# A two-layer graph network: the experts' remainder tile packed, more expert blocks kept on the chip, the second layer's gate and norms by row tile

## The reference, cut to what matters

```
x = x + gatv2(xn) + mix(xn);  x = x + experts0(layernorm(x))   # 16 experts, hidden 512, top 2
xn = layernorm(x)
# second layer: attention over the edges, then gate, norm and slope
skip = xn @ Wskip.T + bskip
g = sigmoid(concat[skip, rst, skip - rst] @ Wgate.T + bgate)    # rst: the attention's result
rst = g * skip + (1 - g) * rst
rst = layernorm(rst) * ln_w + ln_b;  rst = where(rst >= 0, rst, a * rst)
x = x + rst + (mix_out + xn)                                    # mix_out = q @ kv, 8 heads of 32
# causal attention block on layernorm(x)
x1 = layernorm(x);  h = rmsnorm(x1) * ln1_w;  q, k, v from h, with rotary positions
x2 = x1 + attention(q, k, v) @ wo.T;  flat = rmsnorm(x2) * ln2_w
out = sum over the top 2 of 8 experts of w * (silu(flat @ w1.T) * (flat @ w3.T)) @ w2.T   # hidden 682
x = x + x2 + out
```

## Time and profile before

| | us |
|---|---|
| median of 3 runs | 1204.14 |
| lowest and highest | 1200.51, 1206.46 |
| the profiled execution | 1199.38 |
| its span, first to last instruction | 1197.6 |
| PE, PEld, DVE busy | 958.0, 829.1, 857.0 |
| ACT, POOL busy | 465.5, 466.9 |

### The profile page before, as it was taken

The page is one execution under the profiler, slowest core; times in us unless marked ns, Lnnn a source line. Parts: engine busy times, 40 slices in busy tenths (PEclk is TensorE's granted clock), DMA queues, the critical chain, the costliest instruction groups (busy, mean ns, idle before and its releaser), DMA issues. The chain is left out here.

```text
span 1197.6 us, 19285 instructions
## 1 busy us (share of the span) xinstructions
PE 958.0 (80%) x6570; PEld 829.1 (69%) x6570; DVE 857.0 (72%) x1934; ACT 465.5 (39%) x791; POOL 466.9 (39%) x374
## 2 busy tenths in 40 slices
PE   4277999679989889974736999976891894999995
PEld 2256798568878778854735999864691683788884
DVE  5457459869887779887987888584879547655514
ACT  1154565557859577527511111101460260111110
POOL 2437878887787778850002222150000000211104
PEclk9688999889999999997866999997996896899998
DMA  8942232322322222129505999870000002777763
GB/s 284 292 145 69 52 73 55 83 47 60 74 62 58 61 61 69 34 44 245 142 22 192 335 322 323 319 246 22 1 2 0 1 2 71 260 268 264 268 240 93
DMA packets 58236, 157.47 MB, mean 131 GB/s; under 512 B 23830, under 2 KB 33227, under 8 KB 49907
## 3 DMA queue, kind: packets, MB, share of 16 engines
q1 hardware_dynamic: 25500, 116.04, 29.8%
q0 software_dynamic: 25056, 24.10, 9.0%
q10 hardware_dynamic: 7610, 16.46, 4.1%
HBM read 136.12 MB, written 20.12 MB: 130 GB/s over the span
## 5 line engine op out<-in xcount | busy, mean ns | idle before, releaser
L2075 POOL DMA_INDIRECT arena<-row_tab,ids x42 | 57.8, 1376 | 503.2 <-DVE ids L1528 500.6
L2030 POOL DMA_INDIRECT pair_scores<-sc_ring,idx_ring x160 | 213.6, 1335 | 61.9 <-issue 48.0
L750 PE MATMUL bank<-arena 128*128 128x128 f32 (+1 forms) x1616 | 200.6, 282 | 3.2 <-DMA arena<-in_exp 3.2
L750 PEld LDWEIGHTS bank<-arena 128*128 128x128 f32 (+1 forms) x1616 | 188.0, 190 | 12.2 <-DMA arena<-in_exp 4.4
L2020 POOL DMA_INDIRECT arena<-xl_tab,idx_ring x120 | 157.9, 1316 | 91.8 <-issue 37.5
L1763 ACT ACTIVATE arena<-fmaps,node_neg 125x875 f32<-125x875 int32 x100 | 100.2, 1023 | 33.8 <-PE bank L524 14.5
L761 PE MATMUL bank<-arena 128*128 128x256 f32 (+1 forms) x404 | 99.2, 388 | 0.5 <-DMA arena<-in_exp0o 0.5
L1767 ACT ACTIVATE late_ohT<-arena 125x875 fp32r<-125x875 f32 x100 | 90.7, 927 | 0.0
L1899 ACT ACTIVATE arena<-bank 128x512 f32<-128x512 f32 (+2 forms) x76 | 32.4, 450 | 140.9 <-PE bank L750 140.9
L524 PE MATMUL bank<-late_hi,late_ohT 125*125 125x256 f32 x500 | 84.3, 298 | 1.4 <-DVE arena L1000 0.8
L761 PEld LDWEIGHTS bank<-arena 128*128 128x128 f32 (+1 forms) x404 | 72.0, 190 | 17.3 <-issue 9.0
(11 more groups left out here) (330 smaller groups left out, 1977.0 us busy)
## 6 DMA issues: line engine op xcount, KB each, us to landing
arena<-in_exp SPq DMA_DIRECT2D x25, 1024.0 KB
arena<-in_exp SPq DMA_DIRECT2D x17, 1364.0 KB
arena<-in_exp0o SPq DMA_DIRECT2D x25, 512.0 KB
arena<-in_exp1o SPq DMA_DIRECT2D x17, 640.0 KB
fmaps<-in_rows SPq DMA_DIRECT2D x20, 437.5 KB
arena<-pair_scores SPq DMA_DIRECT2D x7, 1093.8 KB
pair_scores<-cnt SPq DMA_DIRECT2D x5, 1093.8 KB
pair_scores<-cnt ACTq DMA_DIRECT2D x5, 1093.8 KB
```

The source lines that it names most:

```text
L750: mm = pe.matmul(banks[1 + 2 * q + buf][0:rows, i * SLOTS:(i + 1) * SLOTS], w_in(s, q, k, m, rows), xsT[:, s, k, :], start=(k == 0), stop= ...
L2030: p.indirect_dma_start(out=pair_scores[which], in_=sc_ring[:, b % 2, j, :], in_offset=None, out_offset=bass.IndirectOffsetOnAxis(ap=idx_ri ...
L2075: p.indirect_dma_start(out=xs[:, q, :], out_offset=None, in_=tab, in_offset=bass.IndirectOffsetOnAxis(ap=ids[:, q, :], axis=0))\
```

## The change

1. **Packed remainder (e1).** The 42 remaining columns of w3 and of w1 stand in one weight tile of 106 columns (w3 in columns 0 to 41, zeros to 63, w1 in 64 to 105). One product of 106 columns takes the place of two of 42. ACT reads w1's part from partitions 64 up, DVE w3's from partition 0 up, in the same bank. The block's weight load grows from 2728 to 2772 columns.
2. **KEPT** is 5 in e0 and 3 in e1. The fifth matrix and result use `mask_words`, so the making of `nmask` and `cnt` moves from e0's end to behind `from_fm("xnT2")`.
3. **Gate.** The third weighted sum is folded into two (weights wg_skip + wg_diff and wg_rst - wg_diff). The skip sums move ahead in `beside_l1`; tiles 0 to 3 are gated at i = 21, with exp, add and reciprocal in place of sigmoid; only tile 4 is left for after the attention.
4. **Norms.** The affine's weight and bias are folded into the passes, x + xn is brought into `cout`'s bank by PE as an identity product, both inverse roots of the double norm are made in one pass (`norm_twice`), and tiles 0 to 2 go ahead of 3 and 4. PE turns and projects chunk 0 when tiles 0 to 2 are there, then chunk 1.
5. **Router.** The rows are multiplied with ln2_w and turned before the inverse root is known; the root is multiplied into the 8 logits on DVE and into the rows on ACT (into `te`, stored from there). x + x2 moves behind `select(3, 1)` of e1.

```diff
-KEPT = {"e0": 4, "e1": 2}
+KEPT = {"e0": 5, "e1": 3}
...
+PACKED = REST_AT + REST1
...
+                                if rows < 128:
+                                    for k in range(K2 if q == 0 else 0):
+                                        pe.matmul(banks[1 + buf][0:PACKED, i * SLOTS:(i + 1) * SLOTS],
+                                                  w_rest(s, k), xsT[:, s, k, :], start=(k == 0), stop=(k == 1))
+                                    continue
...
-            pe.wait_ge(sem("ah"), 1)
-            to_fm("ahT", ta)
-            read_out(pe, "ahT")
-            for name, tiles in (("aq", K2), ("aqr", K2), ("ak", 1), ("akr", 1)):
-                linear_fm(name, fa, name, tiles)
+            for c, (off, w, tiles) in enumerate(CHUNKS):
+                pe.wait_ge(sem("ah"), tiles[-1] + 1)
+                turned(("ahT", c), ta, c)
+                for k in range(K2):
+                    read_out(pe, "ahT", c, k)
...
-                if name == "e0":
-                    for m in range(T):
-                        own.note(v.tensor_scalar(nmask[:, m, :], cnt[:, m, :], -1.0, -BIG, ALU.is_lt, ALU.mult))
...
+                elif i == 21:
+                    gated(1, 0, 1, 2, 3)
...
+            add_prelu(0, 1, 2)
+            norm_twice(0, 1, 2)
+            add_prelu(3, 4)
+            chunk_from_fm("ahT", fa, 0)
+            norm_twice(3, 4)
+            dve.wait_ge(sem("rope_in"), 16)
+            chunk_from_fm("ahT", fa, 1)
+            roped(0)
+            roped(1)
...
+                v.tensor_tensor(ta[:, t, :], tb[:, t, :], Vt(1, "rms2"), ALU.mult).then_inc(sem("weighed"), 1)
```

More of the change, by code:

```diff
@@ L891, in _ @@
             linear_tm("ao", fa, lambda k: W("ao", k), D)
-            pe.wait_ge(sem("flat"), 1)
-            to_fm("flatT", ta)
+            for c, (off, w, tiles) in enumerate(CHUNKS):
+                pe.wait_ge(sem("weighed"), tiles[-1] + 1)
+                turned(("flatT", c), ta, c)
             read_out(pe, "flatT")
@@ L1582, in experts @@
                 select(3, 1)
+                if beside is not None:
+                    beside()
                 block_steps(dve, nblk, step)
[L1584 to L1590 removed]
                 copy_y(nblk - 1, (nblk - 1) % 2)
@@ L1610, in _ @@
             from_fm("xnT2", fa)
+            for m in range(T):
+                own.note(v.tensor_scalar(nmask[:, m, :], cnt[:, m, :], -1.0, -BIG, ALU.is_lt, ALU.mult))
+            own.fence()
+            for m in range(T):
+                own.note(v.scalar_tensor_tensor(cnt[:, m, :], cnt[:, m, :], HD ** 0.5, nmask[:, m, :], ALU.mult,
+                                                ALU.add))
             for c, (off, w, _) in enumerate(CHUNKS):
@@ new lines, in gate_logits, with gated @@
+            def gate_logits(a, b):
+                own.link(v.tensor_tensor(gate[:, a:b], gpart[:, 0, a:b], gpart[:, 1, a:b], ALU.add))
+                v.tensor_scalar(gate[:, a:b], gate[:, a:b], vec[0:P, V_BGATE:V_BGATE + 1], -80.0, ALU.add, ALU.max)\
+                    .then_inc(sem("glogit"), 1)
+            def gated(n, *tiles):
+                a, b = tiles[0], tiles[-1] + 1
+                dve.wait_ge(sem("gated"), n)
+                own.link(v.tensor_scalar(gate[:, a:b], gate[:, a:b], 1.0, None, ALU.add))
+                own.link(v.reciprocal(gate[:, a:b], gate[:, a:b]))
+                for t in tiles:
+                    own.note(v.scalar_tensor_tensor(te[:, t, :], ta[:, t, :], gate[:, t:t + 1], te[:, t, :], ALU.mult,
+                                                    ALU.add))
+                own.fence()
+                for t in tiles:
+                    own.note(v.bn_stats(stats[:, t, :], te[:, t, :]))
@@ L1637, in beside_l1, with centred @@
+            def centred(*tiles):
+                own.fence()
+                for t in tiles:
+                    own.note(v.bn_aggr(mv[:, t, :], stats[:, t, :]))
+                own.fence()
+                for t in tiles:
+                    own.note(v.scalar_tensor_tensor(ta[:, t, :], te[:, t, :], mv[:, t, 0:1], Vt(1, "ln_w"),
+                                                    ALU.subtract, ALU.mult))
             def beside_l1(i):
@@ L1673, in _ @@
                    all_tiles, lambda o, a: v.tensor_scalar(o, a, 1e-30, None, ALU.max), te, beside_l1)
[L1674 to L1677 removed]
+            gate_rest(T - 1)
+            gate_logits(T - 1, T)
             for k in range(K2):
@@ L1681, in _ @@
                     .then_inc(freed, 1)
-            dve.wait_ge(sem("gated"), 1)
-            for t in range(T):
-                own.note(v.scalar_tensor_tensor(te[:, t, :], ta[:, t, :], gate[:, t:t + 1], te[:, t, :], ALU.mult,
-                                                ALU.add))
+            centred(0, 1, 2, 3)
+            gated(2, T - 1)
+            centred(T - 1)
             own.fence()
-            layernorm(te, ta, 1e-5, (sem("ln"), 3 * T))
-            affine(ta, 1, "ln_w", "ln_b", sem("g1"))
@@ L1860, in attend, with gate_exponentials @@
                         turned_out(i - 2)
+                    if name == "l1" and i == len(steps):
+                        gate_exponentials(0, T - 1, 1)
+            def gate_exponentials(first, end, n):
+                act.wait_ge(sem("glogit"), n)
+                a.activation(gate[:, first:end], gate[:, first:end], ACT.Exp, scale=-1.0).then_inc(sem("gated"), 1)
             def elu_exponentials(m):
@@ L1955, in _ @@
             attend("l1", all_tiles)
-            act.wait_ge(sem("glogit"), 1)
-            a.activation(gate[:, :], gate[:, :], ACT.Sigmoid, bias=vec[0:P, V_BGATE:V_BGATE + 1])\
-                .then_inc(sem("gated"), 1)
-            from_fm("ahT", fa)
+            gate_exponentials(T - 1, T, 2)
+            chunks_from_fm("ahT", fa)
             attend("l2", causal_tiles)
             from_fm("yT", fa)
-            from_fm("flatT", fa)
+            chunks_from_fm("flatT", fa)
+            act.wait_ge(sem("flat_root"), 1)
+            for t in range(T):
+                a.activation(te[:, t, :], ta[:, t, :], ACT.Copy, scale=rstd[:, t:t + 1]).then_inc(sem("flat"), 1)
             shares("gate1", NE1)
```

219 lines of the change are left out of this document (147 added, 72 removed).

## The result

The changed kernel takes 1173.33 us (median of 4 runs, 1164.56 to 1175.26), the kernel before beside it 1203.12 us (1200.51 to 1206.46). The ratio is 0.9752, 95% interval 0.9718 to 0.9785: 25.9 to 33.9 us gained, 29.8 by the ratio. Predicted were 27.4 us and 1177, range 1168 to 1189. The profiled execution takes 1172.37 us, its span is 1170.5 (before 1197.6).

What follows compares the result with a forecast made beforehand. PE was taken to bound both expert stretches, DVE the stretch between the attentions. Terms -18.2 - 5.1 + 2.0 - 2.2 - 3.9 = -27.4 us on 1204.14 gave 1176.7, predicted as 1177, range 1168 to 1189.

Steps and rivals of the forecast that it cites:

- e1's end: After e1's blocks: last adds 7.8 us behind PE's outputs instead of 12.9, gathers ending last by 0.9; 5.1 us gained.
- E1's blocks: PE in e1: four fewer instructions and fewer width-change pauses gain 1.07 us a block, 18.2 us over 17 blocks.
- The bet: In e1's products, a 106-column tile counts as full, so pauses beside it vanish; 18.2 us taken.
- the pauses stay: Rival in e1's blocks: pauses remain with 106 columns, gain only 7.6 to 12.9 us, time 1182 to 1188; chance 0.20.
- Transfers: Rival in e1: blocks become bound by transfers, nothing of the 18.2 us seen, time 1195; chance 0.04.
- E0: First expert stretch: fifth kept block brings a new wait, +2.0 us, bounds -1 to +9.
- The chain: In e0, DVE waits some 10 us for fetched rows, delaying block 24's gather; PE's turning comes 3.4 us late.
- Gate, norms, projections: Between the attentions: chunk 0 turned ten us earlier, attention starts at 950.1 instead of 952.73; -2.2 us, from -5 to +1.
- The last rival of the list: Norms: tiles 0 to 2 first gain nothing for projections, chunk 0's copy waiting; costs 2 us at most, 1179.
- Router: Second attention to top 2: top 2 done at 1003.9, -3.9 us, from -4.5 to -3.

Runs made afterwards that it cites:

- experiment 11: The changed kernel with KEPT 4 instead of 5 in e0; 1169.69 us, ratio 0.9751 to the kernel before.
- experiment 1: The changed kernel with e1's remainder unpacked again into two products of 42 columns; 1182.94 us, ratio 0.9854 to the kernel before.
- experiment 5: The changed kernel with e0's two rows stored a step earlier and fetched at the end of step 3 instead of step 20's start; 1167.78 us, ratio 0.9726.
- experiment 7: The changed kernel with slope, add and double norm for all five row tiles at once, not tiles 0 to 2 first; 1170.86 us, ratio 0.9774.
- experiment 8: The changed kernel with chunk 0's rotary passes on DVE ahead of chunk 1's copy; 1168.25 us, ratio 0.9741.
- experiment 6: The changed kernel with KEPT 4 instead of 3 in e1, block 13's share left out of row tiles 0 and 2; 1168.3 us, ratio 0.9721.
- experiment 12: The changed kernel with the gate of all five row tiles behind the attention; 1173.92 us, ratio 0.9787.
- experiment 4: The kernel before with unit 1's order changed, both full products first, then both of 42 columns; 1195.4 us, ratio 0.995.
- experiment 2: The kernel before with the packed remainder alone; 1179.05 us, ratio 0.9796.

## Why the prediction was right

The forecast held, in sum and in its mechanisms; its terms were off by up to 3 us, in both directions. That e1's end gave 1.0 us less and the norms 3.2 more, so that the sum came within 2.4 us of the measured 29.8, is partly luck. By stretches, each profile cut at the same instructions (means; in brackets the profiles and their extremes):

| stretch | before | changed | difference | predicted |
|---|---|---|---|---|
| e0, first hidden product to last adds | 162.1 (5: 159.6 to 163.7) | 163.3 (7: 161.0 to 166.6) | +1.2 | +2.0 |
| to the causal attention | 147.0 (4: 145.4 to 148.0) | 141.6 (6: 140.8 to 142.2) | -5.4 | -2.2 |
| to the top 2 | 55.0 (5) | 50.4 or 52.1 | -4.6 or -2.9 | -3.9 |
| e1, first hidden product to first combining | 156.7 (2: 156.2, 157.1) | 138.9 (10: 138.1 to 139.6) | -17.8 | -18.2 |
| to the last adds | 13.2 (4: 12.9 to 13.5) | 9.1 (7: 7.7 to 11.0) | -4.1 | -5.1 |
| sum | | | -30.7 or -29.0 | -27.4 |

An experiment counts in the column of the part that it has (KEPT 4 of experiment 11 as "before" in e0, experiment 1's blocks as "before" in e1). The ratio says -29.8.

- **E1's blocks: right in mechanism and size.** The bet was that 106 columns count as full. Blocks of 8.08, 8.52, 8.83 and 9.15 us against 8.08, 8.53, 8.89 and 9.15 expected leave the rival "the pauses stay" (8.4 to 8.7 for the changed kernel) no room. The forecast's 0.13 us a change was low, since it spread the hidden part's 0.52 over four changes of which one lies half outside; the sum is the same. The Trainium skill, page TensorEngine Tiling (Array Packing), section Key Properties, has the rule that a change of mode drains the engine; the runs show a price of 0.16 us a change on the mean, and do not show that a drain is what takes it. Transfers did not take over: 295 GB/s and 0.82, predicted 311 and 0.85.
- **E1's end: right in mechanism, 1 us off on the mean, 3.2 in the profiled run.** In the profiled run the gathers end last, as said, but by 4.3 us and not by 0.9. Two terms were too small: from the last store's issue to the first gather 7.8 us in that run and 6.2 to 6.3 in experiments 5, 7 and 8, taken as 5.9 (weights of 1386 and 640 KB are issued 3.1 us and 0.3 us ahead of that store); and the ten gathers took 16.2 us from the first issue to the last instead of 14.8, since three of them met DVE's spreadings. Experiment 6 confirms the other half: with the gathers out of the way PE's combining ends last.
- **E0: right in sign, at the edge of what profiles can tell.** The chain was as described, DVE 7.76 us (10 forecast), PE 4.51 (3.4). But in the other six profiles with KEPT 5 and the late fetch PE's wait before block 24 was 4.3 us, 3.1 us and four times at most 0.2. E0 took 164.4 to 166.6 us in the three profiles with the wait and 161.0 to 163.2 in the four without, so where it shows it is worth some 3 us. A fifth kept block is no gain: experiment 11 has the same ratio without it.
- **Gate, norms, projections: the mechanism right, the size off by 3.2 us, outside its own bounds (-5 to +1).** Turning came 1.4 us earlier than worked out, and the stretch from projections to attention took 22.6 us instead of 24.3: chunk 0 kept PE for 9.8 us (927.75 to 937.57), not 11.1, and chunk 1 followed it at once. The last rival of the list, that the row tile order gains nothing, was half right: the order gave 1.9 us (experiment 7).
- **Router: between the two measured values.** That there are two goes with TensorE's clock. Behind the attention, in 10 us that hold the attention's products with `ao`, the clock stood at 1.00 in three profiles (50.4 us) and at 0.83 in four others of the same program part (52.1 us), by the windows:

```profile
984.21:994.21 10.00, 7.17 (x41) 1.00 0.00 0
```

  That is the changed kernel's window 34 to 44 us behind the attention's start; the columns are the window, its length, PE's busy time and count, PEclk, DMA share, GB/s. The same window of experiment 1:

```profile
976.14:986.14 10.00, 8.19 (x37) 0.83 0.00 0
```

  There the 20 matmul instructions of `ao` took 4.55 and 6.24 us. 1.00 is the level of 2.4 GHz, 0.83 a window in which it fell to that of 1.2. PE's rows ahead of the fall are alike (a turning behind 0.68 us of waiting, `ao` behind 1.05), so no run shows why it fell. Experiments 7 and 12 have this program part too and took 51.5 and 52.6 us: in the first 5 us of their attention the clock stood at 0.66 and 0.69 instead of 1.00, and in experiment 12 it fell under `ao` as well.

## What to carry to other kernels

Look at the shapes that alternate in an engine's program, not only at their number: a row with two shapes and a mean above that of its pure neighbour is a lead, and putting like shapes side by side is a test that costs a few lines. When a stage's blocks get faster, go back to what they hid: one more kept block was worth 6.9 us with blocks of 9.15 us (13.2 to 6.3 behind the outputs) and 4.4 with blocks of 8.08 (13.5 to 9.1); 6.3 and 13.5 are one profile each. And where a queue waits, see what stands behind the waiting copy; moving work that is ready in front of it paid 1.5 us here.

## What the runs showed of the hardware

- A change from a weight tile of 128 columns to one of 42 cost TensorE 0.13 us and the way back 0.19 (start times in the kernel before; 0.16 each by experiment 4); between 106 and 128 columns it costs nothing that the rows show (0.44 us from the first of the four instructions of 106 columns to the next row, 0.44 from the first of the four of 128 behind them).
- A tile of 42 rows costs alike. In the output product of e1 the instructions of 256 columns start 0.216 us apart; into the last tile, of 42 rows, and out of it the distances are 0.308, 0.319 and 0.308, 0.29 us a block more. This is left in the changed kernel too: by an estimate from these distances 4.9 us over 17 blocks, which no experiment tried to take.
- GpSimd's issue of an indirect gather took 1.21 us alone and up to 2.2 us beside one of DVE's spreadings, where mostly one or two gathers of each are longer. The Trainium skill, page SBUF — State Buffer, section SBUF: two separate sides, says that DVE with two inputs from SBUF and a GpSimd instruction that reads SBUF share a pair of ports, which one of them holds for a whole instruction. The rows of experiment 6 agree in that the two gathers beside the spreading take 0.50 and 0.64 us longer; a gather that began 0.90 us ahead of the spreading did not, and no run shows that the ports are the cause.
- From the issue of the last store (128 KB) to the gather that waits for it were 4.0 and 4.2 us with KEPT 2 in e1 (experiment 2, the kernel before) and 5.9 to 7.8 with KEPT 3, where a hidden weight load is issued shortly ahead of the store. That the load makes the difference was not tried by itself and is not shown.
